# Attention in an audio tower: v's projection leaves PSUM by VectorE, and the casts of q and k go to GpSimd

## What is computed

```python
qkv = x @ Wqkv + bqkv
q, k, v = jnp.reshape(qkv, (3, b, n, d, h))
score = jnp.einsum('bnqh,btqh->bnth', q, k) * d ** (-0.5)
attn = jax.nn.softmax(score, axis=1)
av = jnp.einsum('bnnh,bnqh->bnqh', attn, v)
out = av.reshape(b, n, d * h) @ W0 + b0
```

## Time and profile before

| | |
|---|---|
| time, median of 3 runs | 558.85 us (558.7 to 559.1) |
| span of the profiled execution | 558.3 us |
| busy: PE, DVE, ACT, POOL | 378.6, 369.1, 290.4, 273.7 us |
| units 0 to 15 of attention | about 75 to 350 us |

### The profile page before, as it was taken

One profiled execution on the slowest core, in us unless ns is written; L12 is line 12 of the kernel. 1 busy time (PEld: TensorE's weight loads), 2 busy tenths in 40 slices (PEclk: granted clock), 3 DMA queues, 4 the chain that ended last, 5 costly groups with the idle time before them and its releaser, 6 DMA issues.

```text
span 558.3 us, 8700 instructions
## 1 busy us (share of the span) xinstructions
PE 378.6 (68%) x3014; PEld 251.9 (45%) x3014; DVE 369.1 (66%) x596; ACT 290.4 (52%) x652; POOL 273.7 (49%) x316
## 2 busy tenths in 40 slices
PE   1212487888889978899588895475107997487781
PEld 1212353444547645476355652364105775254450
DVE  1295148777887779877878679625774999542431
ACT  1103466999986999869698695101101110144441
POOL 3036385333322468633658613838555777742211
PEclk9999997999999999999989998555557999599996
DMA  3500269839323332223303400380004110200000
GB/s 81 110 1 0 53 150 214 191 71 211 80 53 84 84 82 56 47 67 84 83 4 92 103 1 1 71 142 0 19 13 125 36 44 24 73 9 5 7 5 8
DMA packets 54530, 36.05 MB, mean 65 GB/s; under 512 B 25122, under 2 KB 53687, under 8 KB 54480
## 3 DMA queue, kind: packets, MB, share of 16 engines
q1 hardware_dynamic: 51538, 32.97, 27.7%
q0 software_dynamic: 2944, 2.45, 1.6%
HBM read 10.57 MB, written 8.79 MB: 35 GB/s over the span
## 4 chain that ended last, share of the span: by engine, by line
ACT 29%; PE 27%; DVE 25%; issue 8%; DMA 3%; SPq 3%; POOL 2%; POOLq 0%; DVEq 0%; ACTq 0%
ACT S L884 16%; PE S L697 6%; DVE nm L1031 5%; PE U L643 5%; DVE lm L1203 4%; ACT vT L871 4%; ACT k L871 3%; ACT q L871 3%; DVE vT L1196 3%; PE S L797 3%; PE U L604 2%; DMA vT<-in_L_attn_Wqkv 2%; PE U L797 2%; PE S L799 1%; SPq L282 1%
## 5 line engine op out<-in xcount | busy, mean ns | idle before, releaser
L1031 DVE TENSOR_REDUCE nm<-S 128x1 f32<-128x748 f32 x192 | 171.9, 932 | 44.3 <-PE S L697 41.7
L884 ACT ACTIVATE S<-S,nm 128x748 f32<-128x748 f32 x192 | 166.8, 883 | 42.4 <-DVE nm L1031 41.1
L697 PE MATMUL S<-pool_a 128*128 128x512 f16 (+1 forms) x768 | 151.4, 333 | 28.6 <-ACT S L884 26.0
L697 PEld LDWEIGHTS S<-pool_a 128*128 128x128 f16 x768 | 69.0, 105 | 91.4 <-ACT S L884 57.6
L520 POOL DMA_INDIRECT out<-lm,vT x44 | 43.3, 985 | 58.2 <-DVE lm L1209 51.2
L442 POOL TENSOR_TENSOR pool_a<-q,pool_a 128x750 f16<-128x750 f32 x16 | 25.8, 1610 | 82.4 <-DVE pool_a L1025 82.4
L604 PE MATMUL U<-xhT,wq 128*128 128x250 f16 x288 | 43.4, 292 | 21.0 <-ACT k L871 10.1
L1203 DVE TENSOR_REDUCE lm<-vT 128x64 f32<-128x512 f32 x44 | 45.1, 1026 | 1.3
L604 PEld LDWEIGHTS U<-xhT,wq 128*128 128x128 f16 x288 | 26.9, 104 | 39.6 <-ACT k L871 15.9
L884 ACT ACTIVATION_READ_ACCUMULATOR S<-S,nm 128x1 f32 x192 | 43.5, 226 | 0.0
L1196 DVE TENSOR_TENSOR vT<-vT 128x512 f32<-128x512 f32 x12 | 8.3, 693 | 41.9 <-ACT vT L953 41.9
(11 more groups left out here) (214 smaller groups left out, 666.8 us busy)
## 6 DMA issues: line engine op xcount, KB each, us to landing
pool_a<-pool_a SPq DMA_DIRECT2D x64, 187.5 KB, 3.0
pool_a<-pool_a SPq DMA_DIRECT2D x64, 93.8 KB, 2.8
sorted_rows<-zrow SPq DMA_DIRECT2D x1, 3864.0 KB, 22.6
vT<-sorted_rows SPq DMA_DIRECT2D x11, 276.0 KB, 3.7
w<-in_L_ffn_w2s SPq DMA_DIRECT2D x1, 2048.0 KB
lm<-in_x SPq DMA_DIRECT2D x4, 375.0 KB
pool_a<-in_L_ffn_w2s SPq DMA_DIRECT2D x1, 1024.0 KB
vT<-in_L_attn_Wqkv SPq DMA_DIRECT2D x2, 384.0 KB, 9.3
```

Of the source, the lines that this page charges most:

```text
L697: last = mm(S[n % 3][:, c0:c1], kst[:, u % 3, a, hd, START[t]:START[t] + P], qst[:, u % 3, hd, c0:c1], start=(a == 0), stop=(a == 1))
L884: sc_.activation(S[n % 3][:, 0:N], S[n % 3][:, 0:N], ACT.Exp, bias=nm[:, b % 2, j, i:i + 1], accum_out=sm[:, b % 2, j, i:i + 1]).then_inc( ...
L1031: v.tensor_reduce(nm[:, b % 2, j, i:i + 1], S[n % 3][:, 0:N], X, ALU.max, negate=True).then_inc(s_max, 1)
```

## The change

ACT no longer copies v out of U. DVE does it in `v_out`, behind maximum 6 of each unit: an addition of a tensor (from U) and a bias column that is broadcast. Where the first block of U belongs to another bias column than the others, the addition is made in two pieces; in the second batch it is one. `diag_copy` goes with it. DVE no longer makes the upper halves of q and k; POOL makes them in `qk_lo`, each right ahead of the lower half. The waits are carried over: POOL now waits for the copy out of U and for the transfers that last read the buffer.

```diff
             def qk_lo(w):
                 c = w % 2
                 for n, (src, s_c) in enumerate(((q32, s_qc), (k32, s_kc))):
+                    pool.wait_ge(s_ue, unit_no[("qk"[n], w, 0)] + 1)
+                    if w >= 2:
+                        pool.wait_ge(s_st[(w - 2) % 3], 16 * 8 * ((w - 2) // 3 + 1))
+                    gp.tensor_copy(hl[:, c, n, 0, 0:QN], src[:, c, 0:QN]).then_inc(s_c, 1)
                     pool.wait_ge(s_c, w + 1)
                     gp.tensor_tensor(hl[:, c, n, 1, 0:QN], src[:, c, 0:QN], hl[:, c, n, 0, 0:QN],
                                      ALU.subtract).then_inc(s_lo, 1)
...
-                if kind == "v" and w >= 1:
-                    last = diag_copy(w - 1)
                 last.then_inc(s_ue, 1)
...
-                    if i in (0, 2, 4) and u + AHEAD < NU:
-                        qkv_out("qkv"[i // 2], u + AHEAD)
-                    if i == 4 and u + AHEAD == NU:
-                        act.wait_ge(s_uf, unit_no[("d", NU - 1, 0)] + 1)
-                        diag_copy(NU - 1).then_inc(s_ue, 1)
+                    if i in (0, 2) and u + AHEAD < NU:
+                        qkv_out("qk"[i // 2], u + AHEAD)
...
-            def hi_cast(kind, w):
-                n = "qk".index(kind)
-                dve.wait_ge(s_ue, unit_no[(kind, w, 0)] + 1)
-                if w >= 2:
-                    dve.wait_ge(s_st[(w - 2) % 3], 16 * 8 * ((w - 2) // 3 + 1))
-                v.tensor_copy(hl[:, w % 2, n, 0, 0:QN], (q32, k32)[n][:, w % 2, 0:QN]).then_inc((s_qc, s_kc)[n], 1)
+            def diag_copy(w):
+                b, j = divmod(w, NPAIR)
+                return v.tensor_copy(dg[:, b % 2, j, :], U[:, U_D:U_D + 2 * NT])
+
+            def v_out(w):
+
+                b, j = divmod(w, NPAIR)
+                dve.wait_ge(s_uf, unit_no[("v", w, 0)] + 1)
+                if w >= 8:
+                    dve.wait_ge(s_av, w - 7)
+                g0 = (2 * T + b * N) % 3
+                n_first = 3 - g0
+                parts = [(0, n_first, g0), (n_first, 3, 0)] if g0 else [(0, 3, 0)]
+                dst = vT[:, w % 8, 0:QN].rearrange("p (n s) -> p s n", s=3)
+                for s0, s1, g in parts:
+                    bv = bq[:, g * NPAIR + j:(g + s1 - s0 - 1) * NPAIR + j + 1:NPAIR]
+                    last = v.tensor_tensor(dst[:, s0:s1, :],
+                                           U[:, 256 * s0:256 * s1].rearrange("p (s n) -> p s n", n=256)[:, :, 0:NP3],
+                                           bv.unsqueeze(2).to_broadcast([P, s1 - s0, NP3]), ALU.add)
+                if w >= 1:
+                    last = diag_copy(w - 1)
+                last.then_inc(s_ue, 1)
...
             for w in range(AHEAD):
-                hi_cast("q", w)
-                hi_cast("k", w)
+                v_out(w)
...
-                    if i in (3, 5) and u + AHEAD < NU:
-                        hi_cast("qk"[(i - 3) // 2], u + AHEAD)
+                    if i == 6 and u + AHEAD < NU:
+                        v_out(u + AHEAD)
+                    if i == 6 and u + AHEAD == NU:
+                        dve.wait_ge(s_uf, unit_no[("d", NU - 1, 0)] + 1)
+                        diag_copy(NU - 1).then_inc(s_ue, 1)
```

More of the change, by code:

```diff
@@ L848, in _ @@
             sc_.mul(w1T[0:D, NODES:256], idf[0:D, 0:1], 0.0).then_inc(s_w1c, 1)
-            def diag_copy(w):
-                b, j = divmod(w, NPAIR)
-                if b >= 2 and j == 0:
-                    act.wait_ge(s_ex1, b - 1)
-                return sc_.copy(dg[:, b % 2, j, :], U[:, U_D:U_D + 2 * NT])
             def qkv_out(kind, w):
@@ L861, in qkv_out @@
                 act.wait_ge(s_uf, unit_no[(kind, w, 0)] + 1)
-                if kind != "v" and w >= 2:
+                if w >= 2:
                     act.wait_ge(s_prod, w - 1)
-                if kind == "v" and w >= 8:
-                    act.wait_ge(s_av, w - 7)
-                dst = {"q": q32[:, w % 2, 0:QN], "k": k32[:, w % 2, 0:QN], "v": vT[:, w % 8, 0:QN]}[kind]
+                dst = {"q": q32[:, w % 2, 0:QN], "k": k32[:, w % 2, 0:QN]}[kind]
                 base = "qkv".index(kind) * T + b * N
@@ L906, in _ @@
             for w in range(AHEAD):
-                for kind in "qkv":
+                for kind in "qk":
                     qkv_out(kind, w)
```

## The result

The changed kernel takes 567.45 us (median of 4 runs, 564.5 to 568.24), the kernel before beside it 558.98 us (4 runs, 558.7 to 559.36). The ratio is 1.0139, with a 95% interval from 1.0113 to 1.0165 (the recorded ratio; the two medians alone divide to 1.0152): the change makes the kernel 1.4% slower. The forecast was 564.4 us in a range from 557 to 575.

A forecast was written before the change was run, and what follows sets the result against it. Attention was taken as bound by waits round ACT, PE and DVE, with little slack on DVE, and by the single tile U. -4.3 + 0.25 + 1.0 + 7.9 + 0.65 = +5.5 on 558.85 gave 564.4 us, range 557 to 575.

The forecast's parts named there:

- (b): Casts on POOL: 0.85 us each, start +0.25; pair 2's product at 93.0, needed by PE at about 93.6.
- (e): Units where U is wanted next: later release, nine units at a mean of 0.88, +7.9; unit 14 +0.65.
- (a): Unit 0: casts leave DVE, so none is held by the memset; 19.25 shrinks to 14.99, -4.3 us.
- (c): v's addition on DVE: no penalty for its three-float output step; DVE kept 1.03 us, copy done after 1.10.
- (d): Plain units 1, 2, 3, 7: v's addition ahead of maximum 7 delays exponential 7; +0.24 us each, 1.0 for four.
- Dear addition: Rival on v's addition: 2.0 ns an element keeps DVE 1.75 us, not 1.03; +10, 574.5 us; chance 0.17.
- POOL is too slow: Rival: POOL casts of 1.61, or DVE's diagonal-weight operations waiting behind POOL's; 568 us; chance 0.05.
- The release of U is hidden: Rival: PE reaches U's broadcast late anyway, so those units cost only +0.24; 558 us, no change; chance 0.08.
- ACT's relief is worth its length: Rival: 13 units each get 1.26 us shorter, 538 us; half of it, 547; chance in full or part 0.18.

The follow-up runs named there:

- e10_early_all: The changed kernel with v's addition behind maximum 5, zeros written in four parts, and w7's memset at POOL's start: 554.36 us, ratio 0.9910.
- e6_early_split: The changed kernel with v's addition behind maximum 5 and the zeros written in four parts behind pairs 1 to 4: 555.13 us, ratio 0.9919.
- e7_memset: The kernel before, with only w7's memset moved from unit 0 to POOL's idle start: 557.8 us, ratio 0.9964.
- e3_v_only: The kernel before, with only v and the diagonal copy moved to DVE behind maximum 6, casts staying on DVE: 592.09 us on a slower chip, ratio 1.0088.
- e8_before_split: The kernel before, with w7's memset at POOL's start and the zeros written in four parts: 555.38 us, ratio 0.9925.
- e1_again: The changed kernel once more, no edit, on a slower chip: 590.1 us, ratio 1.0061.
- e2_casts_only: The kernel before, with only the q and k casts moved to POOL, v still on ACT: 583.38 us on a slower chip, ratio 0.9963.
- e5_early: The changed kernel with v's addition and the diagonal copy behind maximum 5 instead of 6: 557.72 us, ratio 0.9965.
- e9_unit_step: The changed kernel with v's addition writing results one behind the other, not at a step of three floats (output differs): 567.77 us, ratio 1.0142.
- e4_zeros_split: The changed kernel with the write of zeros cut into four parts behind pairs 1 to 4: 587.24 us on a slower chip, ratio 1.0017.
- e12_zeros_split: The same kernel as e4_zeros_split, timed again on a chip where the kernel before takes 559.64 us: 563.0 us, ratio 1.0057.
- e11_early_dve_casts: As e10_early_all, but with the q and k casts back on DVE behind maxima 3 and 4: 560.23 us, ratio 1.0007.

## Why the prediction was right, and where it was not

Slower, with 564.4 in the middle, was right; the profiled run took 564.5, the median 567.45. The main loss is the one forecast, a later release of U. That the profiled run meets the forecast to 0.1 us is in part luck: unit 1 lost 1.3 us (under (b)) and the table stage was 1.5 us shorter (under (e)), neither of them in the forecast.

**(a) The stall of unit 0.** Forecast -4.3, measured 14.94 - 19.24 = -4.30. In that profile unit 0 starts at 79.20, late enough for pair 2's product. In the seven profiles described under (b) it starts earlier, PE waits for the product, and the unit takes 15.3 to 15.6; e10_early_all, where the product does not wait for the memset, has 14.39 against 15.43 in e6_early_split. e7_memset shows the cause: the memset's place alone brings unit 0 to 14.76, e3_v_only keeps the long cast.

**(b) The casts on POOL.** Taken at 0.85, they take 0.809 (803 to 831 ns). The start shifts by 0.16 (q copy of unit 0 at 79.20 instead of 79.04), forecast 0.25; but other profiles start unit 0 at 78.0 to 78.6 with the casts on POOL and at 78.21 and 78.47 with them on DVE (e7_memset, e8_before_split), so such a shift is not shown. Pair 2's product was forecast at 93.0 and comes at 91.06 + 1.76 = 92.8; in the first profile nobody waits for it, but in e1_again PE's diagonal does:

```profile
93.07 0.61 PE L619 MATMUL U<-sel,qk 128*128 128x2 f32 x4 [0.43 <-POOL qk L450]
```

In seven profiles with the casts on POOL and the memset in its old place, unit 0 starts at 78.0 to 78.6 and this wait is 0.20 to 0.98 us; e10_early_all, where the memset is out of the way, is free of it. The step that failed is the last sentence of (b): "The transfers that SyncE issues behind these casts are wanted only a unit later still." They are, but they queue behind the write of zeros, and a unit 0 that is 4.3 shorter uses up just the slack that had hidden it. Measured: 16.25 - 14.93 = 1.3 us in the first profile, 2.6 in e1_again; and, each against the plain units of its own kernel, 3.3 in e2_casts_only, 3.1 in e7_memset, 2.9 in e5_early and 6.0 in e9_unit_step. e4_zeros_split and e12_zeros_split bring it to zero, so the cause is shown: the one large write ahead. Whether it holds the stacks up by its place in the queue or by the load on the DMA engines (their share is 1.16 in the window from 90 to 97 us) was not tried apart. The Trainium skill, page "DMA: Bandwidth & Descriptors", section on queues, rings and completion order, says that a DMA engine takes up what is in a ring in the ring's order; the traces agree in that the transfers issued behind all the zeros are late and those issued behind a quarter of them are not. Beyond it, the issue itself took 5.48 us behind the zeros and 0.48 behind a quarter of them (e12_zeros_split).

Part of that price is the clock. Windows of 108 to 112 us, right behind the wait, of e7_memset and then of the changed kernel's first profile:

```profile
108.00:112.00 4.00, 4.00 (x21) 2.72 (x20) 1.95 (x3) 2.11 (x5) 0.00 (x0) 0.62 0.27 82
```

```profile
108.00:112.00 4.00, 3.56 (x28) 2.38 (x27) 2.96 (x4) 2.55 (x7) 0.14 (x1) 1.00 0.44 115
```

In e7_memset PE waited 2.01 us (the weight load 2.4, for the stacks), its granted clock was at 0.62 on average behind it, partly at the lower level of 1.2 GHz, and 21 matmuls filled the window; in the first profile the wait was 1.62 and the clock stayed at 1.00, with 28 matmuls not filling it. e1_again, with 1.46 us of waiting and a clock of 0.69 behind it, says that the length of this one wait does not decide alone. In the profiles in which it fell, unit 1 lost 1.1 to 1.4 us more than PE's wait was long (2.9 by a wait of 1.84 in e5_early, 6.0 by 4.62 in e9_unit_step); in the first, in which it did not, 1.3 by 1.62. A longer wait and a fallen clock together may be why three of the four runs of the changed kernel lie 2.4 to 3.7 us above the profiled one. It is argued from other profiles, since those three have none, and it has a rival: the profiled run's table stage was 0.5 to 3.3 us shorter than that of any other profile on chips of this pace (under (e)), and other runs need not have that. e12_zeros_split lowers the median by about 4.6 us and leaves the spread nearly as it was. So the cause of the spread stays open.

**(c) The addition.** Forecast 1.03 on DVE and released after 1.10; measured 1.11 and 1.19. The pieces were forecast at 0.67 and 0.41 and took 0.81 and 0.48. The step "three is nearer to two, so I take none" was wrong: the step of three floats costs a factor of 1.3, far from the upper end of 2.0 ns (1.36). The Trainium skill, page "SBUF — State Buffer", Specifications, has the right sign here, full speed at two accesses in a line of 16 bytes and less below; it gives no price.

**(d) Plain units.** Forecast +0.24, measured +0.16 or +0.17 in units 2, 3 and 7, in spite of the longer addition. The unit took up 0.15 more than reckoned, and that the addition counts at the margin is seen in e9_unit_step: 0.24 less of it makes a plain unit 0.19 shorter.

**(e) Units that want U.** Forecast a mean of +0.88; units 4, 5, 6 and 8 to 12 sum to +6.91, a mean of 0.86. The order by kind was off: 0.92 to 0.99 in units 4, 8 and 12, 0.79 and 0.81 in 5 and 9, 0.56 and 0.58 in 6 and 10, and 1.28 in unit 11. Not all of the last is the release of U: in that unit PE stands still for 5.5 us before the change and 6.1 after it, its granted clock is 0.50 to 0.52 in the next 4 us, and e7_memset and e8_before_split, with v on ACT, have 21.54 and 21.78 there against 21.24. Units 13 to 15 together lose 1.13, forecast for 13 and 14 0.88 + 0.65. Up to the last exponential (350.8 before, 356.7 after) the parts sum to 0.16 - 4.30 + 1.49 + 3 x 0.17 + 6.91 + 1.13 = 5.90, against a forecast of 5.5. In this one profile the table stage then is 1.5 us shorter, 206.0 instead of 207.5. e9_unit_step, which has v in the same place, has 207.4; e5_early, e7_memset, e8_before_split and e10_early_all have 207.4 to 207.7, e12_zeros_split 206.5, e6_early_split 208.2 and e11_early_dve_casts 209.3. So this stage varies from profile to profile, and nothing shows that the change shortens it. It hid what unit 1 cost, and made the forecast look better than its sum was.

The base of the sum was off too. The forecast compared a span of 558.3 with a median of 558.85 of other runs. In all later profiles an execution's own time is 1.7 to 2.2 us above its span, so the profiled execution of before was probably about 1 us longer than that median, to which its lengths were added.

**The rivals.** *Dear addition* and *POOL is too slow* have something true in them, the factor of 1.3 and the late product, and neither reaches its price in the changed kernel (the wait for the product, priced at 0.9, is at most 0.56 there, and 0.98 in e5_early). *The release of U is hidden* falls by the 1.48 us ahead of the broadcast. *ACT's relief is worth its length* (half of it sums to 546, not 547) falls for this placement, and returns in part in e5_early: plain units of 14.37 are 0.39 under the kernel before, a third of the 1.26 that ACT no longer does. The forecast named the limit rightly (DVE), and missed that one tile earlier it has room. That the casts gain nothing on POOL holds for the changed kernel (e3_v_only), and does not for e10_early_all (e11_early_dve_casts). *POOL is too slow* said also that DVE's small operations would wait behind POOL; they do (1.67 instead of 0.21), and in e2_casts_only, which has only the casts moved, unit 4 is 0.19 longer. How the remaining 0.16 of unit 4 in e5_early come about was not tried apart.

**The lines that were to show it.** q copies 14.92 to 14.94 apart (15.0 forecast), no DVE instruction near 4.9 us at 80, full clock in 90 to 97, the broadcast of unit 5 2.09 behind maximum 6 (2.1), ACT's idle time ahead of exponentials up by 21.5 us (about 20).

## What to carry to other kernels

Work that moves from one engine to another takes a new place in that engine's order, and the place can weigh more than the engine: the same addition costs 0.2 to 1 us a unit behind maximum 6 and gains 0.4 in plain units behind maximum 5, where the engine would have waited for the next scores (units 4 and 8 still lose 0.4 there). Before moving work because a stage looks overloaded, look for the one long instruction: e8_before_split, which moves a memset and a write of zeros and neither a cast nor an addition, has about four fifths of what the fastest kernel here gains (0.75% against 0.90%), and their intervals overlap. When a stall is taken away, list every transfer that had been landing under it, and look at what stands ahead of it in its queue.

## What the hardware showed that was not expected

- VectorE writing f32 with a step of 12 bytes takes 1.36 ns an element, against 1.04 with a step of 4 (e9_unit_step). The fixed part of a piece is about 0.14 us in both.
- POOL casts 750 elements from f32 to f16 in 0.809 us, against 0.54 on DVE and 1.61 for POOL's own subtraction of the same size.
- A small multiplication on DVE with both operands in SBUF (48 elements) took 1.67 us beside a POOL subtraction and 0.21 without, and a DVE cast with one operand 1.79 instead of 0.54. The Trainium skill, page "SBUF — State Buffer", section "SBUF: two separate sides", states that of a shared pair of ports the one that starts first has it for a whole instruction, and counts operations with two SBUF inputs among those that need it when POOL reads SBUF. The traces agree: the multiplication began 0.01 us behind POOL's subtraction and ended 0.07 behind it.
- The wait of unit 1 for the same eight transfers behind the same 3.9 MB varied between profiles, with a loss from 1.3 to 6.0 us. What sets it within a run stays open.
- On another chip the kernel before took 587 us. The four profiles taken there have attention units of equal length, but a table stage 24 to 26 us longer than in the first profile of the changed kernel (206.0). Why was not tried.
- e11_early_dve_casts had runs from 554.48 to 562.2 us. Its q copy of unit 13, at 299.62, comes 3.7 us later than that of e10_early_all, and its median is 5.9 higher; its table stage is 1.6 longer. The run of 554.48 has a mean granted clock of 0.917, the other nine 0.895 to 0.903; what raises it in one run stays open.
